# Two graph edge sums: a one-column memset on GpSimd ahead of each gather, and semaphores counted once per four slots

## The chip, the cores and the metric

The kernel runs on one core of a Trainium2 chip. The metric is the device time of one execution in microseconds (us). Before the change three runs took 3500.52, 3505.85 and 3508.72 us; the median is 3505.85 us.

The engines are called by the names of the profile: PE is the matrix engine (PEld its weight loads), DVE the vector engine, ACT the scalar engine, POOL the GpSimd engine, SP the engine that only issues transfers here. POOL also issues the indirect DMAs, the transfers that pick rows by an index.

## The reference

A graph of 6250 nodes with 256 features each and 100000 weighted edges goes through four parts. Cut to what matters here:

```
edge_index = stack([src, dst])
x = x + gnn0(layernorm(x))     # segment_sum(w * (ln(x) @ W)[dst], src), batch norm, relu
x = x + ffn0(layernorm(x))     # top-k tokens through a gelu MLP
x = x + gnn1(layernorm(x))     # segment_sum(w * ln(x)[dst], src) + ln(x), MLP, row norm
x = x + ffn1(layernorm(x))     # mixture of 8 experts, 2 per token
```

The two edge sums are the two `segment_sum`s: for each of 100000 edges a row of 256 floats is fetched by the edge's one end, multiplied with the edge's weight, and added to the row of its other end.

## The kernel before, in words

**Chunks and slots.** The 6250 nodes are 49 tiles (`NT`) of 128 rows. The edges are sorted by the tile that they add to and cut into 784 chunks (`CHUNKS`) of 128 edges. A chunk whose edges belong to two tiles has to be used twice, so there are 832 slots (`SLOTS`): one slot is one chunk's part for one tile. Both edge sums run through `aggregate`, the first with `through_mlp` false (its buffers and semaphores are named `g0_`), the second with it true (`g1_`). Every loop in it is unrolled when the program is built. What the trace calls `g_...` is either.

**What each engine does.** POOL issues one indirect DMA for each chunk (line 1089): 128 rows of 1 KB from the table in HBM into one place of `got`, a ring of 56 places (`RING`). DVE makes for each slot a 128x128 matrix `route` that holds the edge's weight in the column of its target row (line 1098). PE multiplies `route` with the chunk's rows into half of a PSUM bank (line 1182; an f32 product is two MATMUL records in the trace). DVE adds that half bank to the tile's row in `A` (line 1115). 16 slots (`GB`) make a step, in four groups of four (`GSEM`). After each step about one tile is complete, and ACT, PE and DVE take it through what follows: in the first sum a product and column statistics, in the second an MLP, two norms and router scores. There are 52 steps (`STEPS`).

**What sets the order.** Each engine runs its own list of instructions in order, and semaphores tie the lists together. `gathered` tells PE that four chunks have landed. `routed` tells PE that four matrices are made. `pairs_summed` counts each second product on PE: DVE waits for it before it adds, and POOL waits for it before it overwrites a place of the ring. `added` counts each addition: DVE waits for it before its next addition, since two slots can add to the same tile, PE waits for it before it reuses a half bank, and ACT waits for it before it takes a finished tile. PE may run at most 14 slots (12 in the second sum) ahead of the additions.

**The ring's wait.** Chunk c takes the place of chunk c-56. A chunk can still be used up to 48 slots after its own number, so before gathers c and c+1 POOL waits until the products of all slots up to c-7 are done (`last_user`, `done`). The wait is carried by a semaphore instruction of its own (`pool.sem_inc(dma_open, 1)`), once for every two gathers. From chunk 56 on it counts; for chunks 32 and up there is another wait because the eight `gathered` semaphores are reused.

Of the kernel before, what the change touches and what calls it, by code (L numbers as in the profile page):

```python
# [5 lines left out]
ALU = mybir.AluOpType  # L6
# [4 lines left out]
U32 = mybir.dt.uint32  # L11
# [3 lines left out]
P = 128  # L15
# [3 lines left out]
NT = -(-N // P)  # L19
# [64 lines left out]
def wait(engine, sem, value):  # L84

    if not (isinstance(value, int) and value <= 0):
        engine.wait_ge(sem, value)


def build(nc, x, src, dst, edge_weight, g0_w, g0_bias, g0_gamma, g0_beta, f0_wr_in, f0_br, f0_w1, f0_b1_in, f0_w2, f0_b2_in,  # L90
# [14 lines left out]
    with ctx:  # L105
        def sem(name):
            return ctx.enter_context(nc.semaphore(name))
# [5 lines left out]
        dma_open = sem("indirect_dma_open")  # L113
# [897 lines left out]
        def aggregate(rows, name, through_mlp, source, local, weight):  # L1011
# [3 lines left out]
            BANKS = 6 if through_mlp else 7  # L1015
            GROUPS_OF = GB // GSEM
            FINISHES = STEPS - 1
            with ExitStack() as scope, nc.Block() as block:
                here = lambda what, shape, dt=F32: sb(name + what, shape, dt, scope)
                got = here("got", [P, RING, D])  # L1020
                route = here("route", [P, GB + GSEM, P])
                added = sem(name + "added")
                routed, pairs_summed = sem(name + "routed"), sem(name + "pairs_summed")
                tiles_of = GraphTiles(here) if through_mlp else NodeRows(here)
                edges = None if through_mlp else EdgeFields(here)

# [4 lines left out]
                def first_slot_after(q):  # L1031

                    return next(first for first in range(0, SLOTS, GSEM) if landed_by(first) >= q)
# [41 lines left out]
                @block.gpsimd  # L1075
                def _(pool):
                    for q in range(CHUNKS // GSEM):
                        if not through_mlp and q * GSEM in (0, 4 * P):
                            pool.wait_ge(edges.sources_made, 1 + (q > 0))
                        for half in range(2):  # L1080
                            first = q * GSEM + half * (GSEM // 2)
                            last_user = first + GSEM // 2 - 1 - RING + (NT - 1)
                            done = last_user // 2 + 1 if first >= RING else 0
                            if q >= 8:
                                done = max(done, first_slot_after(q - 8) // 2 + 1)
                            wait(pool, pairs_summed, done)
                            pool.sem_inc(dma_open, 1)
                            for c in range(first, first + GSEM // 2):
                                pool.indirect_dma_start(  # L1089
                                    got[:, c % RING, :], None, rows,  # L1090
                                    bass.IndirectOffsetOnAxis(ap=source[:, c:c + 1].bitcast(U32), axis=0)
                                ).then_inc(gathered[q % 8], 16)

                @block.vector
                def _(dve):
# [6 lines left out]
                    def add_sums(n, g):  # L1102
                        first = n * GB + g * GSEM
                        _, tiles = nc.values_load_multi_w_load_instructions(
                            slot_tile[0:1, first:first + GSEM], engines=(mybir.EngineType.DVE,), min_val=0, max_val=NT - 1,
                            skip_runtime_bounds_check_because="the map is clamped to the tiles")
                        if n + 1 < STEPS:
                            make_routes(n + 1, g)
                        for j in range(GSEM):
                            c = first + j  # L1110
                            to = row(A, tiles[j])
                            if j % 2 == 0:
                                dve.wait_ge(pairs_summed, c // 2 + 1)
                            dve.wait_ge(added, c + 1)
                            dve.tensor_tensor(to, to, sums_of(c), ALU.add).then_inc(added, 1)  # L1115

                    if not through_mlp:
                        edges.make(dve)
# [42 lines left out]
                def _(pe):  # L1161
# [5 lines left out]
                    for n in range(STEPS):  # L1167
                        u = n % 2
                        for g in range(GROUPS_OF):
                            pe.wait_ge(routed, n * GROUPS_OF + g + 1)  # L1170
                            first = n * GB + g * GSEM
                            for q in range(asked[0], landed_by(first) + 1):
                                pe.wait_ge(gathered[q % 8], gathered_after(q))
                            asked[0] = landed_by(first) + 1
                            _, at = nc.values_load_multi_w_load_instructions(
                                slot_ring[0:1, first:first + GSEM], engines=(mybir.EngineType.PE,), min_val=0, max_val=RING - 1,
                                skip_runtime_bounds_check_because="the ring's places are below its size")
                            for j in range(g * GSEM, (g + 1) * GSEM):
                                c = n * GB + j
                                if c % 2 == 0 and c >= 2 * BANKS:  # L1180
                                    pe.wait_ge(added, c - 2 * BANKS + 3)
                                ins = pe.matmul(sums_of(c), route[:, c % (GB + GSEM), :], row(got, at[j % GSEM]), start=True, stop=True)  # L1182
                                if c % 2 == 1:
                                    ins.then_inc(pairs_summed, 1)
                            if through_mlp and n >= 2 and g == 0:
                                tiles_of.second_product(pe, n - 2)
                            if through_mlp and n >= 4 and g == 0:
                                tiles_of.score(pe, n - 4)
                            if n >= 1 and g == 1:
                                tiles_of.turn(pe, n - 1)  # L1190
                            if n >= 1 and g == (3 if through_mlp else 2):
                                tiles_of.first_product(pe, n - 1)
                            if through_mlp and n >= 3 and g == 3:
                                tiles_of.turn_normal(pe, n - 3)
# [17 lines left out]
                def _(act):  # L1212
                    if through_mlp:
                        act.wait_ge(tiles_of.loaded, tiles_of.LOADS * 16)
                    for n in range(1, STEPS):
                        act.wait_ge(added, n * GB + 1)
                        t = tile_to_finish(n, mybir.EngineType.Activation)
                        tiles_of.tile.stage(act, n - 1, t)
                        if through_mlp:
# [15 lines left out]
                    if through_mlp:  # L1235
                        tiles_of.keep_result(act, FINISHES - 1)
                        tiles_of.keep_scores(act, FINISHES - 3, tile_to_finish(FINISHES - 2, mybir.EngineType.Activation))
                        left = last_tile(act)
                        act.wait_ge(added, SLOTS + 1)
                        tiles_of.tile.stage(act, FINISHES, left)  # L1240
                        tiles_of.root_of(act, FINISHES - 1)
                        tiles_of.keep_turned(act, FINISHES)
# [10 lines left out]
                        tiles_of.keep_normal_turned(act, FINISHES)  # L1253
                        tiles_of.keep_scores(act, FINISHES, left)
                    else:
                        act.wait_ge(added, SLOTS + 1)
                        left = last_tile(act)
                        tiles_of.tile.stage(act, FINISHES, left)
                        tiles_of.keep_turned(act, FINISHES)
# [968 lines left out]
```

## Time and profile before

| | before |
|---|---|
| median of 3 timed runs | 3505.85 us |
| the profiled execution, first to last instruction | 3891.6 us |
| PE busy | 2650.3 us |
| DVE busy | 2586.9 us |
| POOL busy | 2179.1 us |
| gathers of both edge sums (line 1089) | 1568, busy 1493.5 us, POOL idle before them 845.0 us |
| first and last gather of both sums start at | 369.8 and 3110.5 us |

The profiled execution is 386 us longer than the median of the timed ones, because recording the trace takes time of its own. Nothing else around its span is told, so the span stands for its own time. A row of a group reads: line, engine, operation, what it writes and reads, how many; behind the first bar the busy time in us and the mean of one in ns; behind the second the engine's idle time just before such instructions and what ended most of it. "issue" is idle time that no semaphore explains, "remote" a semaphore whose giver the trace can't name.

### The profile page before, as it was taken

Reading aid. Unit: us, or ns where it says so; the run is one execution under the profiler, and the core shown is the slowest. Engines: PE = TensorE matmul, PEld = TensorE weight load, DVE = VectorE, ACT = ScalarE, POOL = GpSimd, SP = SyncE. Lnnn points to the kernel's source line nnn. Section 1 sums busy time; section 2 is a strip of 40 time slices with the busy share of each in tenths; the row PEclk is TensorE's granted clock in tenths of the full one; section 3 lists DMA queues with packets and bytes.
Section 4 is the critical chain, followed back from the end, with each engine's and each line's share of the span. In section 5 each row is a group of like instructions: output and inputs, shape, how many; then the busy total and the mean of one; then the engine's idle time right before and its main releaser. Section 6 shows DMA issues by size and latency. Waiting matters only on the chain. (4 is left out here: it accounts for less than half of the span.)

```text
span 3891.6 us, 55224 instructions
## 1 busy us (share of the span) xinstructions
PE 2650.3 (68%) x15016; PEld 2238.8 (58%) x15016; DVE 2586.9 (66%) x6599; ACT 1024.1 (26%) x2120; POOL 2179.1 (56%) x2145
## 2 busy tenths in 40 slices
PE   6886555444454545789946666666666657999998
PEld 4666343333343434689935444444444537999998
DVE  8997655444554555976746566666666677888886
ACT  0021000000000000567501111111111127888886
POOL 1434566666666664335456666666666603666665
PEclk8998777777777777899967777777887768999999
DMA  3011333333333332000133333333333334776775
GB/s 90 4 46 58 102 91 92 91 91 88 91 92 88 92 88 63 12 1 23 55 90 96 96 96 96 96 96 94 98 95 94 95 103 165 216 216 212 213 215 146
DMA packets 164219, 387.69 MB, mean 100 GB/s; under 512 B 46324, under 2 KB 95528, under 8 KB 150561
## 3 DMA queue, kind: packets, MB, share of 16 engines
q0 software_dynamic: 99072, 233.49, 22.0%
q1 hardware_dynamic: 64929, 151.65, 11.4%
q8 instruction: 94, 1.54, 0.2%
q14 instruction: 124, 1.02, 0.1%
HBM read 342.69 MB, written 42.97 MB: 99 GB/s over the span
## 5 line engine op out<-in xcount | busy, mean ns | idle before, releaser
L1089 POOL DMA_INDIRECT g_got<-table,e_source x1568 | 1493.5, 952 | 845.0 <-issue 440.0
L1115 DVE TENSOR_TENSOR A<-A,psum 128x256 f32 x1664 | 698.6, 420 | 876.3 <-remote 532.0
L1182 PE MATMUL psum<-g_got,g_route 128*128 x3328 | 1034.7, 473 | 141.0 <-DMA g_got<-table,e_source 74.2
L1182 PEld LDWEIGHTS psum<-g_got,g_route 128*128 128x128 f32 x3328 | 771.9, 241 | 329.0 <-issue 198.4
L786 PE MATMUL psum<-ident,g_rows 128*128 128x128 f32 x208 | 63.0, 401 | 663.3 <-ACT A L834 410.2
L1098 DVE TENSOR_SCALAR g_route<-columns,e_local,e_weight 128x128 f32<-128x128 f32 x1664 | 471.6, 362 | 17.4 <-issue 12.2
L786 PEld LDWEIGHTS psum<-ident,g_rows 128*128 128x128 f32 x208 | 29.7, 190 | 703.8 <-ACT A L834 505.7
L834 ACT COPY A<-psum 128x256 f32 x52 | 19.3, 372 | 999.4 <-issue 637.4
L369 POOL DMA_INDIRECT records<-rec,place x120 | 120.6, 1005 | 233.7 <-ACT rec L585 159.1
L140 PE MATMUL psum<-e_xt_hi,e_w_hi 128*128 128x256 f32 x832 | 238.2, 286 | 5.4 <-issue 5.2
L1612 POOL TENSOR_TENSOR f_ht_lo<-f_ht,f_ht_hi 128x512 fp32r<-128x512 f32 x100 | 134.2, 1347 | 181.1 <-ACT f_ht_hi L1551 174.6
L140 PE MATMUL psum<-e_w_hi,e_ht_hi 128*128 128x256 f32 x832 | 232.8, 280 | 3.1 <-DVE e_w_lo L2011 3.1
L141 PE MATMUL psum<-e_xt_lo,e_w_hi 128*128 128x256 f32 x832 | 233.8, 281 | 0.0
L142 PE MATMUL psum<-e_xt_hi,e_w_lo 128*128 128x256 f32 x832 | 233.7, 281 | 0.0
L141 PE MATMUL psum<-e_w_lo,e_ht_hi 128*128 128x256 f32 x832 | 232.6, 280 | 0.0
L142 PE MATMUL psum<-e_w_hi,e_ht_lo 128*128 128x256 f32 x832 | 232.4, 279 | 0.0
L655 PE MATMUL psum<-to_row,value 125*48 125x128 f32 x1600 | 199.2, 288 | 40.4 <-DVE to_row L553 35.9
L655 PEld LDWEIGHTS psum<-to_row,value 125*48 125x48 f32 x1600 | 187.8, 131 | 64.3 <-issue 49.2
L1890 POOL DMA_INDIRECT out<-e_y,e_homes x104 | 177.0, 1702 | 63.4 <-POOL e_homes L1886 47.6
L2156 ACT ACTIVATE e_ht<-psum,e_b 128x256 f32<-128x256 f32 x416 | 181.7, 472 | 100.2 <-PE psum L142 100.1
L2017 DVE TENSOR_TENSOR e_ht_lo<-e_ht,e_ht_hi 128x512 fp32r<-128x512 f32 x208 | 138.9, 690 | 52.9 <-ACT e_ht_hi L2160 44.8
L140 PEld LDWEIGHTS psum<-e_xt_hi,e_w_hi 128*128 128x128 f32 x832 | 157.7, 190 | 5.8 <-issue 5.8
(413 smaller groups left out, 5403.5 us busy)
## 6 DMA issues: line engine op xcount, KB each, us to landing
e_w<-in_m_w SPq DMA_DIRECT2D x104, 1024.0 KB, 5.1
g_got<-table,e_source POOLq DMA_INDIRECT x1568
expert_table<-g_normal SPq DMA_DIRECT2D x52, 128.0 KB
table<-xn SPq DMA_DIRECT2D x49, 128.0 KB
X<-in_x SPq DMA_DIRECT2D x1, 6144.0 KB
table<-f_ring SPq DMA_DIRECT2D x24, 256.0 KB, 2.1
out<-X SPq DMA_DIRECT2D x1, 6144.0 KB
f_w<-in_f_w SPq DMA_DIRECT2D x2, 1024.0 KB, 6.5
```

The source lines that it names most:

```text
L140: pe.matmul(to, a_hi, b_hi, start=first, stop=False)
L141: pe.matmul(to, a_hi, b_lo, start=False, stop=False)
L142: return pe.matmul(to, a_lo, b_hi, start=False, stop=last)
L655: ins = pe.matmul(sums_of(u), value[0:EP, u, j, :, :].rearrange("p f c -> p (f c)"), to_row[0:EP, u, j, :], start=j == 0, stop=j == GC - 1)
L1089: pool.indirect_dma_start(got[:, c % RING, :], None, rows, bass.IndirectOffsetOnAxis(ap=source[:, c:c + 1].bitcast(U32), axis=0)).then_inc ...
L1098: ins = dve.tensor_scalar(route[:, (n * GB + j) % (GB + GSEM), :], columns[:], local[:, n * GB + j:n * GB + j + 1], weight[:, n * GB + j:n ...
L1115: dve.tensor_tensor(to, to, sums_of(c), ALU.add).then_inc(added, 1)
L1182: ins = pe.matmul(sums_of(c), route[:, c % (GB + GSEM), :], row(got, at[j % GSEM]), start=True, stop=True)
L1612: pool.tensor_tensor(ht_lo[:, m % 2, of], ht[:, of], ht_hi[:, m % 2, of], ALU.subtract).then_inc(h_split, 1)
L1890: pool.indirect_dma_start(out, bass.IndirectOffsetOnAxis(ap=homes[:, u, j:j + 1].bitcast(U32), axis=0), y[:, u, j, :], None, bounds_check= ...
L2017: dve.tensor_tensor(ht_lo[:, u, of], ht[:, of], ht_hi[:, u, of], ALU.subtract).then_inc(h_split, 1)
L2156: act.activation(ht[:, b * MT:(b + 1) * MT], psum[:, 1 + b % 4, 0:MT], ACT.Gelu, bias=b1[:, one, b]).then_inc(hid_out, 1)
```

## The change

In both edge sums:

- POOL: before each gather `memset` writes 0.0 to one column of a scratch tile `pause` (128 rows, one float each). Each gather has its own column. Nothing reads it. That is 784 memsets in each sum, 1568 in all.
- POOL: the ring's wait and the semaphore instruction that carries it stand once for four gathers. The wait before gathers c to c+3 is for the products up to slot c-5, all of them before the first of the four.
- PE: the products are counted once per four (`groups_summed`) and no longer once per two.
- DVE: it waits once per four additions for the products and for its own last group; between the four additions stands a `drain`, and `added` is counted once per four.
- PE's wait for half banks and ACT's wait for a finished tile are restated in the new unit. The first covers one group, rounded up.

```diff
+                pause = here("pause", [P, CHUNKS])
...
-                        for half in range(2):
-                            first = q * GSEM + half * (GSEM // 2)
-                            last_user = first + GSEM // 2 - 1 - RING + (NT - 1)
-                            done = last_user // 2 + 1 if first >= RING else 0
-                            if q >= 8:
-                                done = max(done, first_slot_after(q - 8) // 2 + 1)
-                            wait(pool, pairs_summed, done)
-                            pool.sem_inc(dma_open, 1)
-                            for c in range(first, first + GSEM // 2):
-                                pool.indirect_dma_start(
+                        first = q * GSEM
+                        last_user = first + GSEM - 1 - RING + (NT - 1)
+                        done = last_user // GSEM + 1 if first >= RING else 0
+                        if q >= 8:
+                            done = max(done, first_slot_after(q - 8) // GSEM + 1)
+                        wait(pool, groups_summed, done)
+                        pool.sem_inc(dma_open, 1)
+                        for c in range(first, first + GSEM):
+                            pool.memset(pause[:, c:c + 1], 0.0)
+                            pool.indirect_dma_start(
...
+                        dve.wait_ge(groups_summed, first // GSEM + 1)
+                        dve.wait_ge(added, first // GSEM + 1)
                         for j in range(GSEM):
-                            c = first + j
                             to = row(A, tiles[j])
-                            if j % 2 == 0:
-                                dve.wait_ge(pairs_summed, c // 2 + 1)
-                            dve.wait_ge(added, c + 1)
-                            dve.tensor_tensor(to, to, sums_of(c), ALU.add).then_inc(added, 1)
+                            if j > 0:
+                                dve.drain()
+                            ins = dve.tensor_tensor(to, to, sums_of(first + j), ALU.add)
+                        ins.then_inc(added, 1)
...
-                                    pe.wait_ge(added, c - 2 * BANKS + 3)
+                                    pe.wait_ge(added, (c - 2 * BANKS + 1) // GSEM + 2)
                                 ins = pe.matmul(sums_of(c), route[:, c % (GB + GSEM), :], row(got, at[j % GSEM]), start=True, stop=True)
-                                if c % 2 == 1:
-                                    ins.then_inc(pairs_summed, 1)
+                            ins.then_inc(groups_summed, 1)
```

POOL in the middle of the first edge sum, before. A row is one gather; what it waits for stands in brackets.

```order
L1089 DMA g_got<-table,e_source 128x256 [waits g0_pairs_summed]
L1089 DMA g_got<-table,e_source 128x256
L1089 DMA g_got<-table,e_source 128x256 [waits g0_pairs_summed]
L1089 DMA g_got<-table,e_source 128x256
L1089 DMA g_got<-table,e_source 128x256 [waits g0_pairs_summed]
```

The same place now:

```order
L1089 MEMSET g_pause 128x1 [waits g0_groups_summed]
L1090 DMA g_got<-table,e_source 128x256
L1089 MEMSET g_pause 128x1
L1090 DMA g_got<-table,e_source 128x256
L1089 MEMSET g_pause 128x1
L1090 DMA g_got<-table,e_source 128x256
L1089 MEMSET g_pause 128x1
L1090 DMA g_got<-table,e_source 128x256
L1089 MEMSET g_pause 128x1 [waits g0_groups_summed]
```

Every gather now has a memset in front of it, and the wait stands ahead of every fourth gather and no longer ahead of every second.

DVE at the first group of the first edge sum, before. ISA is the register instruction that sets the address of the tile to add to.

```order
L1104 TENSOR_LOAD slot_tile
L1098 TENSOR_SCALAR g_route<-columns,e_local,e_weight 128x128 x4
L1115 ISA [waits g0_added,g0_pairs_summed]
L1115 TENSOR_TENSOR A<-A,psum 128x256
L1115 ISA [waits g0_added]
L1115 TENSOR_TENSOR A<-A,psum 128x256
L1115 ISA [waits g0_added,g0_pairs_summed]
L1115 TENSOR_TENSOR A<-A,psum 128x256
L1115 ISA [waits g0_added]
L1115 TENSOR_TENSOR A<-A,psum 128x256
```

The same place now (the drains between the additions are not listed in this view):

```order
L1105 TENSOR_LOAD slot_tile
L1099 TENSOR_SCALAR g_route<-columns,e_local,e_weight 128x128 x4
L1116 ISA [waits g0_added,g0_groups_summed]
L1116 TENSOR_TENSOR A<-A,psum 128x256
L1116 ISA
L1116 TENSOR_TENSOR A<-A,psum 128x256
L1116 ISA
L1116 TENSOR_TENSOR A<-A,psum 128x256
L1116 ISA
L1116 TENSOR_TENSOR A<-A,psum 128x256
```

The instructions stand in the same order; of five semaphore conditions behind the first one none is left.

## Rows read from the trace of the kernel before

**Rows 1.** The page, part 1: busy time of each engine

```profile
PE 2650.3 (68%) x15016; PEld 2238.8 (58%) x15016; DVE 2586.9 (66%) x6599; ACT 1024.1 (26%) x2120; POOL 2179.1 (56%) x2145
```

**Rows 2.** The line of the gathers, L1089: durations min/median/max, idle time before, by releaser

```profile
L1089 POOL DMA_INDIRECT g_got<-table,e_source x1568: 940/946/1200, 369.8 to 3110.5; - x196
...
  issue: 440.0, 1415
  remote: 246.6, 74
```

**Rows 3.** Timeline, all engines, 793 to 812 us: start, length, what, [idle before <-releaser]

```profile
793.60 5.35 PE L1182 MATMUL psum<-g_got,g_route 128*128 x24
...
801.40 0.95 POOL L1089 DMA_INDIRECT g_got<-table,e_source  x1 [0.30 <-issue]
802.66 0.95 POOL L1089 DMA_INDIRECT g_got<-table,e_source  x1 [0.30 <-issue]
806.55 0.98 DVE L1115 TENSOR_TENSOR A<-A,psum 128x256 f32 x2 [9.35 <-remote]
807.20 0.95 POOL L1089 DMA_INDIRECT g_got<-table,e_source  x1 [3.59 <-remote]
```

**Rows 4.** Timeline of POOL, 0 to 6 us: memsets of one column in a row

```profile
0.26 0.10 POOL L2220 MEMSET const-float32-1.0<- 128x1 f32 x1
0.29 0.10 POOL L2220 MEMSET const-bfloat16-1.0<- 128x1 bf16 x1
```

**Rows 5.** Timeline of POOL, 3223 to 3256 us, the expert part's start

```profile
3226.62 1.82 POOL L1903 DMA_INDIRECT e_rows<-expert_table,e_nodes  x1 [0.31 <-issue]
3228.45 0.19 POOL L1899 COPY e_nodes<-node_of 128x2 int32<-128x2 int32 x1
3229.46 0.97 POOL L1903 DMA_INDIRECT e_rows<-expert_table,e_nodes  x1 [0.82 <-POOL e_nodes L1899]
...
3233.93 0.18 POOL L1899 COPY e_nodes<-node_of 128x2 int32<-128x2 int32 x1 [2.25 <-DVE e_xt_lo L2037]
```

**Rows 6.** Groups by line and shape, POOL, the expert part: busy us, mean ns

```profile
L1903 POOL DMA_INDIRECT e_rows<-expert_table,e_nodes x104 | 114.1, 1097 | 62.1 <-POOL e_nodes L1899 45.1 <-issue 16.4 <-DMA out<-e_y,e_homes 0.6
L1899 POOL COPY e_nodes<-node_of 128x2 int32 x47 | 55.4, 1178 | 0.0
```

**Rows 7.** Timeline of POOL where the ring first fills, first and second sum

```profile
463.09 1.03 POOL L1089 DMA_INDIRECT g_got<-table,e_source  x1 [16.41 <-PE psum L1182]
...
473.26 0.94 POOL L1089 DMA_INDIRECT g_got<-table,e_source  x1 [0.33 <-issue]
```

```profile
2040.14 0.94 POOL L1089 DMA_INDIRECT g_got<-table,e_source  x1 [9.83 <-PE psum L1182]
```

**Rows 8.** Timeline, all engines, 474 to 486 us

```profile
477.01 0.95 POOL L1089 DMA_INDIRECT g_got<-table,e_source  x1 [0.30 <-issue]
...
480.35 1.99 PE L1182 MATMUL psum<-g_got,g_route 128*128 x8 [0.92 <-DMA g_got<-table,e_source]
480.97 0.95 POOL L1089 DMA_INDIRECT g_got<-table,e_source  x1 [3.01 <-PE psum L1182]
```

**Rows 9.** Timeline of DVE, 455 to 485 us

```profile
457.07 0.98 DVE L1115 TENSOR_TENSOR A<-A,psum 128x256 f32 x2
458.26 0.98 DVE L1115 TENSOR_TENSOR A<-A,psum 128x256 f32 x2 [0.21 <-DVE A L1115]
...
460.27 0.98 DVE L1115 TENSOR_TENSOR A<-A,psum 128x256 f32 x2
```

**Rows 10.** The line of the additions, L1115, durations min/median/max

```profile
L1115 DVE TENSOR_TENSOR A<-A,psum x1664: 405/420/425, 418.6 to 3147.3; 128x256 f32 x185
```

**Rows 11.** Windows: length, PE, PEld, DVE, ACT, POOL busy (instructions), PE clock, DMA share, GB/s

```profile
700.00:1400.00 700.00, 334.69 (x1304) 272.26 (x1303) 354.03 (x1055) 35.63 (x93) 454.90 (x481) 0.73 0.31 90
2100.00:3000.00 900.00, 594.21 (x2120) 440.33 (x2120) 572.38 (x1803) 98.74 (x353) 587.62 (x613) 0.78 0.33 96
```

**Rows 12.** Groups by line, DVE, 2100 to 3000 us

```profile
L1115 DVE TENSOR_TENSOR A<-A,psum 128x256 f32 x629 | 263.7, 419 | 256.3 <-remote 88.2 <-PE psum L1182 86.1 <-DVE A L1115 27.2
```

More of the change, by code:

```diff
@@ L1020, in aggregate @@
                 got = here("got", [P, RING, D])
+                pause = here("pause", [P, CHUNKS])
                 route = here("route", [P, GB + GSEM, P])
                 added = sem(name + "added")
-                routed, pairs_summed = sem(name + "routed"), sem(name + "pairs_summed")
+                routed, groups_summed = sem(name + "routed"), sem(name + "groups_summed")
                 tiles_of = GraphTiles(here) if through_mlp else NodeRows(here)
@@ L1079, in _ @@
                             pool.wait_ge(edges.sources_made, 1 + (q > 0))
-                        for half in range(2):
-                            first = q * GSEM + half * (GSEM // 2)
-                            last_user = first + GSEM // 2 - 1 - RING + (NT - 1)
-                            done = last_user // 2 + 1 if first >= RING else 0
-                            if q >= 8:
-                                done = max(done, first_slot_after(q - 8) // 2 + 1)
-                            wait(pool, pairs_summed, done)
-                            pool.sem_inc(dma_open, 1)
-                            for c in range(first, first + GSEM // 2):
-                                pool.indirect_dma_start(
-                                    got[:, c % RING, :], None, rows,
-                                    bass.IndirectOffsetOnAxis(ap=source[:, c:c + 1].bitcast(U32), axis=0)
-                                ).then_inc(gathered[q % 8], 16)
+                        first = q * GSEM
[8 more added lines that the diff above has]
+                            pool.indirect_dma_start(
+                                got[:, c % RING, :], None, rows,
+                                bass.IndirectOffsetOnAxis(ap=source[:, c:c + 1].bitcast(U32), axis=0)
+                            ).then_inc(gathered[q % 8], 16)
                 @block.vector
@@ L1215, in _ @@
                     for n in range(1, STEPS):
-                        act.wait_ge(added, n * GB + 1)
+                        act.wait_ge(added, n * GROUPS_OF + 1)
                         t = tile_to_finish(n, mybir.EngineType.Activation)
@@ L1238, in _ @@
                         left = last_tile(act)
-                        act.wait_ge(added, SLOTS + 1)
+                        act.wait_ge(added, SLOTS // GSEM + 1)
                         tiles_of.tile.stage(act, FINISHES, left)
@@ L1255, in _ @@
                     else:
-                        act.wait_ge(added, SLOTS + 1)
+                        act.wait_ge(added, SLOTS // GSEM + 1)
                         left = last_tile(act)
```

## The prediction

> **What bounds the kernel now.** I read the page first. Its busy shares point at PE and DVE, with POOL behind them [rows 1], but they average parts with different limits, so I went to the two edge sums by windows: there DVE is busy 51% and 64%, PE 48% and 66%, POOL 65% in both, and the DMA engines a third [rows 11]. No engine is full, so the waits decide. The line of the gathers tells what POOL does: a gather takes 946 ns, and POOL sits idle 845 us before the 1568 of them [rows 2]. The timeline splits that idle time in two. Between gathers that follow at once there is a gap of 0.30 us, so one starts every 1.25 us, as the first two gathers of the timeline show [rows 3]. On 1415 gathers nothing explains the gap; it belongs to the gather. The rest is waits, some 845 - 1568 x 0.305 = 367 us, and most of it has one form: every 12 to 16 gathers, about once a step, POOL stands still for 3.6 us, and DVE for 9.35 us, until PE's counts arrive, although PE's 24 records for those products end at 798.95 and the wait ends at 806.5 [rows 3].
>
> Are those waits there in a timed run? The profiled execution is 3891.6 - 3505.85 = 386 us longer than the median. The gathers' waits are 367 us. The last quarter of the kernel, the expert part, has PE busy nearly throughout and can't give 386 us back. So I take it that late counts from PE are a cost of recording, and that a timed run goes through both edge sums at POOL's own pace: 1568 x 1.25 = 1960 us of the 3506. The sum below is therefore made against the median, 3505.85, and not against the span: in the profiled execution a slower gather would first eat into the 3.6 us waits.
>
> **The memsets.** 1568 more POOL instructions, each in line ahead of a gather, on the engine that sets the pace. No row has a memset between two gathers, so it is bounded. From above: a one-column memset lasts 0.10 us, and the copy of two columns at 3228.45 starts at the moment the gather before it ends, without the 0.30 us gap, and takes 0.19, as much as one that starts on an idle POOL (0.18) [rows 4, 5]. So a small operation neither hides behind a gather nor pays the gap: it adds its length, and the gap stays with the gather. The gather behind such a copy took 0.97 in place of 0.946 [rows 2, 5]. That gives 0.01 + 0.10 + 0.02 = 0.13 us. From below: of memsets in a row each starts 0.03 us after the last [rows 4], so POOL may be free for the gather after 0.03, which gives 0.04 us. The middle, 0.08 us, is what I take. Wider ends: if the memset fits into the 0.30 us gap and the gather then starts at once, the pair gets 0.30 - 0.10 = 0.20 us shorter; if changing between two kinds of work costs what it seems to cost in the expert part's loop (gathers 1097 ns in the mean against 946, copies 1178 against 190 [rows 5, 6]), it gets 0.15 us to about 0.4 us longer.
>
> The Trainium skill bears on this (GPSIMD Engine Reference, "2.1 Instruction dispatch"): each of GpSimd's eight cores starts the next instruction as soon as its own share of the last is done, and a dispatch costs tens of cycles. By it the memset would cost near the lower end, 0.04 us, and the sum below would be some 60 us smaller. The copy that starts at once agrees with the first half; no row here tells the second for a memset.
>
> How many of them count: the first 56 gathers of each sum run into an empty ring and then wait, 16.41 us and 9.83 us [rows 7], and 56 x 0.08 = 4.5 us of memsets only shortens that wait. 1456 are left, and 1456 x 0.08 = 116 us.
>
> **The coarser waits of POOL.** Before, the wait ahead of gathers c, c+1 reached to slot c-7 and the next to c-5; now the first of four waits to c-5, two slots more, 2.5 us earlier in the stream than it had to. It matters only where POOL is close ahead of PE, from chunk 56 to about 71, four groups. The chain is: last gather of a group starts, its product starts 3.3 us later (477.01 to 480.35), four products take 2.0 to 3.8 us, and the next gather starts 0.6 to 0.8 us after the count [rows 8]: 5.9 to 7.9 us, where five gathers give 6.25 us of cover. A stall of 0 to 1.6 us, four times: 0 to 6 us a sum. Before the same chain with two products less just closed, a gap of 0.33 in place of 0.30 [rows 7]. Later each 17 slots give one chunk more of a lead, and nothing waits. With one group more at the ring's first fill (1 to 3 us) I take 5 us a sum, 10 us in all; ends 2 and 20.
>
> **Counts and drains.** PE gives half as many counts and DVE half as many waits. Two additions last 0.98 us for 2 x 0.42 us, so a wait on one's own count costs 0.14 us, and 0.21 us where PE's count is awaited too [rows 9, 10]. If a drain costs nothing, a group of four gets 0.07 to 0.49 us shorter; if it costs as much as the wait, 0.07 us. None of it is on the path while POOL paces the sums. The first sum's DVE needs 3.2 us for a group of four slots, 457.07 to 460.27 [rows 9], where POOL needs 4.7. In the second sum it is close: 572.4 us busy and about 150 us of its own short gaps over some 40 steps (82 of the 150 before the additions [rows 11, 12]) make 18 us a step, POOL's 15.1 gathers 18.9. DVE is the cover here: if it is gone, the second sum can't run faster than today by more than 0.5 to 0.9 us a step. I cost this part at 0; ends -5 and +5.
>
> On the counts the Trainium skill speaks against a gain (VectorE: DVE Perf Modes, "The DRAIN you can't avoid"): eight copies with a semaphore after each took as long as eight with one after the last. By it the edit gives nothing; the row's 0.07 us between the two kinds of wait would be all there is. Both leave the sum as it is.
>
> **Sum.** 116 + 10 + 0 = 126 us. 3505.85 + 126 = 3632 us, 3.6% more.
>
> **Rivals.**
> 1. *The gap closes.* The 0.30 us before each gather is idle time of POOL that no semaphore explains. If part of it belongs to two gathers meeting back to back, a memset between them takes its place. For it: nothing else in the trace explains the gap. Against it: the copy that starts with no gap and is followed by a gather with a gap again, though that one also waits for a semaphore [rows 5]. With 0.10 us gained of the gap: first sum 728 x 0.10 = 73 us, second at DVE's limit about 21 us (52 steps x 0.4), less 10 for the waits: 3505.85 - 84 = 3422 us. With all 0.20 us: 3350 us.
> 2. *The memset is hidden.* It takes 0 to 0.03 us of POOL's time, as the starts in rows 4 allow, or the second sum runs at DVE's pace. 0 to 44 us plus 10: 3516 to 3560 us.
> 3. *Changing work is dear.* Each switch between memset and gather costs 0.15 to 0.4 us, as the expert part's loop suggests. Against it: the copies outside the loop take 0.18 to 0.19 us right beside gathers [rows 5]. 1512 x 0.2 = 302 us at a likely 0.2: about 3820 us; 4120 at the end.
> The point that decides between slower and not is a memset that adds less than 0 us to the 1.25 us period; at -0.007 us it pays for the coarser waits.
>
> **How the numbers follow.** The forecast's mechanism (0.04 to 0.13 us, 3568 to 3715 us) gets 0.55, rival 1 0.22, rival 2 0.13, rival 3 0.10. The likeliest is 3632 us. The range goes from 3420 to 3715 us: it holds the forecast, rival 2, and the nearer part of rival 1, and leaves out rival 3 and the far part of rival 1, some 0.2. The likeliest case's own range is 3568 to 3715. 0.2% is about what a measurement of this kernel can tell, 7 us. Faster by more: rival 1 and a sliver of 2, 0.23. Within: 0.04. Slower: 0.73.
>
> **What would show it.** In the changed profile: memsets of about 0.10 us right at the end of each gather; the start of one gather to the next 1.29 to 1.38 us where nothing waits (1.25 now); gathers still 0.94 to 0.97 us. POOL's wait of 3.6 us once a step shrinks by 16 x 0.08 = 1.3 us, so that the profiled span grows far less than the timed one, to 3890 to 3960 us. Additions on DVE 0.56 us apart or less. The forecast is wrong if the start-to-start time is below 1.26 us (rival 1 or 2) or above 1.4 us (rival 3), or if it is 1.33 us and the time has not moved: then POOL doesn't pace the timed run, and my reading of the 386 us is what failed.

## The result, and the profile after

The changed kernel takes 3512.83 us (median of 20 runs, 3508.55 to 3519.70). The kernel before takes 3509.59 us beside it (20 runs, 3500.52 to 3512.93). The ratio is 1.0013, with a 95% interval of 1.0007 to 1.0019: slower by 0.13%, some 4 us, which is less than the 0.2% taken as no change. (The ratios here are not the quotients of the two medians, which would be 1.0009 for this pair.) The forecast was 3632 us, with 3568 to 3715 for its own mechanism, and the measured time lies outside that. It lies inside the whole range of 3420 to 3715 us, which was wide enough to hold rival 2 and part of rival 1; a time within 0.2% had been given a chance of 0.04. The outcome is near that of rival 2, the hidden memset, with the cost of the coarser waits left over.

The profiled execution spans 3506.7 us and is one of the timed executions, 3508.55 us by its own clock. So recording adds nothing here that can be seen. One chip used below gives the kernel before 3919 us in timed runs, and its trace looks like that of before; the others give it 3504 to 3510 us. The 3891.6 us of the trace before are therefore most likely real time under such a condition, and not stretched by recording, as the text ahead of the prediction has it. Times are compared on one chip only.

The page of after, part 1, answers to [rows 1]. The instructions are the same but for POOL, which has 1568 more.

```profile
PE 2628.2 (75%) x15016; PEld 2217.2 (63%) x15016; DVE 2598.1 (74%) x6599; ACT 1028.1 (29%) x2120; POOL 2374.8 (68%) x3713
```

Part 5 of the same page, four groups of the edge sums: busy us, mean ns, then the engine's idle time before them.

```profile
L1090 POOL DMA_INDIRECT g_got<-table,e_source x1568 | 1495.3, 954 | 288.3 <-issue 274.2
L1184 PE MATMUL psum<-g_got,g_route 128*128 x3328 | 1086.3, 484 | 651.6 <-DMA g_got<-table,e_source 481.3
...
L1116 DVE TENSOR_TENSOR A<-A,psum 128x256 f32 x1664 | 699.2, 420 | 516.3 <-PE psum L1184 298.2
L1099 DVE TENSOR_SCALAR g_route<-columns,e_local,e_weight 128x128 f32<-128x128 f32 x1664 | 470.9, 362 | 18.0 <-issue 12.7
```

The lines of the gathers and of the memsets answer to [rows 2] (durations min/median/max in ns, first and last start; below, idle time by releaser). First the gathers:

```profile
L1090 POOL DMA_INDIRECT g_got<-table,e_source x1568: 942/949/1186, 369.7 to 2755.4; - x196
...
  issue: 274.2, 1438
  PE psum L1184: 1.5, 8
```

Then the memsets:

```profile
L1089 POOL MEMSET g_pause<- x1568: 99/118/372, 369.0 to 2755.1; 128x1 f32 x196
```

Two things are to be seen. The "remote" idle time of 246.6 us is gone, and the last gather starts at 2755.4 in place of 3110.5. That is not the change's work: the kernel before with nothing but the memsets added shows the same (below, last gather at 2749.6), and so does the kernel before with nothing but POOL's wait edited and no memsets (last gather at 2753.7), both near the time of the kernel before. And the idle time that no semaphore explains fell from 440.0 to 274.2 us while 1568 memsets of 0.12 us came in. The memsets lie inside the old gap. The timeline of POOL shows it, where [rows 3] had two gathers 1.26 us apart (start, length, what, idle before):

```profile
461.09 0.95 POOL L1090 DMA_INDIRECT g_got<-table,e_source  x1 [0.19 <-issue]
462.04 0.12 POOL L1089 MEMSET g_pause<- 128x1 f32 x1
462.35 0.94 POOL L1090 DMA_INDIRECT g_got<-table,e_source  x1 [0.19 <-issue]
```

The memset starts at the gather's end, as forecast. The next gather starts 0.31 us after that same end, as without a memset: 461.09 to 462.35.

Where the ring first fills, the coarser waits show ahead of the first of four gathers (here the waiting instruction is the memset), in the place of [rows 7]:

```profile
440.07 0.10 POOL L1089 MEMSET g_pause<- 128x1 f32 x1 [0.37 <-PE psum L1184]
440.73 0.95 POOL L1090 DMA_INDIRECT g_got<-table,e_source  x1 [0.56 <-issue]
...
445.65 0.10 POOL L1089 MEMSET g_pause<- 128x1 f32 x1 [0.21 <-PE psum L1184]
446.31 0.95 POOL L1090 DMA_INDIRECT g_got<-table,e_source  x1 [0.56 <-issue]
...
451.68 0.10 POOL L1089 MEMSET g_pause<- 128x1 f32 x1 [0.66 <-PE psum L1184]
452.33 0.95 POOL L1090 DMA_INDIRECT g_got<-table,e_source  x1 [0.56 <-issue]
```

Behind a memset that waited, the gather starts 0.56 us after the memset's end and not 0.19. The gather before ran from 438.76 to 439.70, so 440.73 is 1.03 us after its end, where 0.31 is usual. So there are three stalls of 0.7, 0.6 and 1.0 us in the first sum; in the second, at 1840.63 and 1852.63, two of 1.3 and 1.9 us. Together 5.5 us. The 16.41 and 9.83 us that POOL waited before chunk 56 in [rows 7] are gone as well: 0.7 us is left in the first sum and nothing in the second. So the first 56 memsets of a sum have no wait to hide in, and all 1568 count.

DVE at the same kind of place as [rows 9], with a drain between two additions:

```profile
779.92 0.42 DVE L1116 TENSOR_TENSOR A<-A,psum 128x256 f32 x1 [3.42 <-PE psum L1184]
780.51 0.42 DVE L1116 TENSOR_TENSOR A<-A,psum 128x256 f32 x1 [0.17 <-issue]
781.10 0.42 DVE L1116 TENSOR_TENSOR A<-A,psum 128x256 f32 x1 [0.17 <-issue]
```

With a drain the next addition starts 0.17 us after the last, between the 0.14 of a wait on one's own count and the 0.21 of a wait on PE's. A group of four has three such gaps, 0.51 us now and 0.14 + 0.21 + 0.14 = 0.49 us before, so the four semaphore conditions fewer (not five, as the text on the change counts them) buy nothing. Additions start 0.59 us apart, where 0.56 or less had been forecast. The longest wait of DVE near the same place is 3.42 us, where [rows 3] has 9.35. There DVE waited on after PE's 24 product records had ended; here PE's 24 records run from 776.15 to 783.23, and the first addition comes at 779.92, while they still go on. The windows inside the two sums answer to [rows 11]; columns are the length, then busy us and instructions of PE, PEld, DVE, ACT and POOL, the granted clock, the DMA share, GB/s:

```profile
700.00:1340.00 640.00, 411.46 (x1410) 310.67 (x1409) 392.05 (x1148) 39.09 (x102) 547.06 (x1020) 0.79 0.37 105
1800.00:2700.00 900.00, 640.22 (x2535) 491.65 (x2535) 685.25 (x2151) 123.32 (x419) 765.79 (x1423) 0.85 0.39 111
```

POOL has 1020 instructions in 640 us, 510 pairs: one pair each 1.255 us. In the second sum it is one each 1.265 us (1423 instructions in 900 us). Apart from the stalls above, POOL goes at nearly its own pace through both sums.

### The profile page after: what moved, and what is told of

The parts are those of the page before. It is cut to its first block and busy times, and to the rows that moved or that the text cites. A ratio compares the mean times of both kernels' runs of the same rounds, so it can differ in the third digit from the quotient of the medians.

```text
span 3506.7 us, 57232 instructions
## 1 busy us (share of the span) xinstructions
PE 2628.2 (75%) x15016; PEld 2217.2 (63%) x15016; DVE 2598.1 (74%) x6599; ACT 1028.1 (29%) x2120; POOL 2374.8 (68%) x3713
## 5 line engine op out<-in xcount | busy, mean ns | idle before, releaser
L1090 POOL DMA_INDIRECT g_got<-table,e_source x1568 | 1495.3, 954 | 288.3 <-issue 274.2
L1184 PE MATMUL psum<-g_got,g_route 128*128 x3328 | 1086.3, 484 | 651.6 <-DMA g_got<-table,e_source 481.3
L1184 PEld LDWEIGHTS psum<-g_got,g_route 128*128 128x128 f32 x3328 | 761.8, 240 | 896.9 <-issue 771.0
L1089 POOL MEMSET g_pause<- 128x1 f32 x1568 | 198.1, 126 | 29.8 <-POOLq L1270 17.3
L2004 DVE TENSOR_TENSOR e_w_lo<-e_w,e_w_hi 128x2048 fp32r<-128x2048 f32 x52 | 119.2, 2293 | 58.3 <-ACT e_w_hi L2166 57.0
```

The source lines that it names most:

```text
L1089: pool.memset(pause[:, c:c + 1], 0.0)
L1090: pool.indirect_dma_start(got[:, c % RING, :], None, rows, bass.IndirectOffsetOnAxis(ap=source[:, c:c + 1].bitcast(U32), axis=0)).then_inc ...
```

## The experiments

**The memset alone** (kernel before plus the memsets).

```diff
                             for c in range(first, first + GSEM // 2):
+                                pool.memset(pause[:, c:c + 1], 0.0)
                                 pool.indirect_dma_start(
```

> The kernel before with the 1568 memsets alone; waits and counts as before. Theory A (the memset fits into the 0.30 us between two gathers): timed within 0.1% of before, 3506 to 3514 us; one gather starts 1.25 us after the last. Theory B (memset costs about 0.08 us and the coarser counts give as much back): 3590 to 3640 us. For the profiled span: if the memsets ended the 3.6 us waits once a step it is near 3510 us, if the halved counts did it stays near 3890 us, which I think likelier.

Measured 3505.18 us (11 runs) beside 3504.43 us of the kernel before (21 runs, measured together with the first four kernels): ratio 1.0001, 0.9991 to 1.0010. Its line of memsets, then that of its gathers:

```profile
L1090 POOL MEMSET g_pause<- x1568: 98/118/279, 368.8 to 2749.3; 128x1 f32 x196
```

```profile
L1091 POOL DMA_INDIRECT g_got<-table,e_source x1568: 942/946/1174, 369.5 to 2749.6; - x196
```

1568 memsets in front of 1568 gathers cost nothing that can be measured: 0.7 us in all, with an interval of -3 to +3.5 us, or 0.000 us each within 0.002. The gathers have no stall where the ring fills. The span is 3503.3 us, not the 3890 thought likelier; the kernel with the counts alone, next, spans 3500.2. So neither half of the change ended the long waits of the trace before: they were never in these runs.

**The counts alone** (changed kernel without the memsets).

```diff
                         for c in range(first, first + GSEM):
-                            pool.memset(pause[:, c:c + 1], 0.0)
                             pool.indirect_dma_start(
```

> The changed kernel without the memsets; counts once per four, drains. Theory A: timed like before, 3506 to 3516 us, and the 3 us by which the changed kernel is slower is split between this and the memsets. Theory B: 3400 to 3430 us. The profiled span is near 3507 us if the halved counts of PE ended the waits in the trace, near 3890 us if the memsets did.

Measured 3509.00 us, ratio 1.0008, 0.9998 to 1.0017. The stalls where the ring fills are there without memsets:

```profile
440.85 0.95 POOL L1089 DMA_INDIRECT g_got<-table,e_source  x1 [0.93 <-PE psum L1183]
...
446.56 0.94 POOL L1089 DMA_INDIRECT g_got<-table,e_source  x1 [0.91 <-PE psum L1183]
...
452.07 0.94 POOL L1089 DMA_INDIRECT g_got<-table,e_source  x1 [0.80 <-PE psum L1183]
```

The two halves of the change add up, 1.0001 and 1.0008 against 1.0013, and the small loss sits in the second half, though its interval just reaches 1. Which line it is, the kernels with one part alone say further below.

**Four memsets ahead of each gather** (changed kernel).

```diff
-                            pool.memset(pause[:, c:c + 1], 0.0)
+                            for m in range(4):
+                                pool.memset(pause[:, 4 * c + m:4 * c + m + 1], 0)   # pause: 4 * CHUNKS bytes a row
```

> The changed kernel with four one-column memsets (one byte wide) ahead of each gather in place of one. Theory A: four in a row end some 0.19 us after the gather (0.10 + 3 x 0.03), inside the 0.30 us gap: no change against the changed kernel, 3513 us, within 0.2%. If each costs its full length one after another, 0.40 to 0.48 us, 0.1 to 0.2 us a gather stick out: 3660 to 3800 us.

Measured 3583.12 us, ratio 1.0219, 1.0197 to 1.0241: 79 us more than before on that chip. Timeline of POOL:

```profile
699.34 0.95 POOL L1091 DMA_INDIRECT g_got<-table,e_source  x1
700.28 0.20 POOL L1090 MEMSET g_pause<- 128x1 uint8 x4
700.63 0.95 POOL L1091 DMA_INDIRECT g_got<-table,e_source  x1
```

Neither expectation was met: theory A said no change, and the other said 3660 us or more. Four memsets take 0.20 us together, and the gather starts 0.35 us after the last gather's end, 0.15 us after the memsets'. From one gather to the next it is 1.296 us where nothing waits, 0.045 more than 1.251, and 0.045 x 1568 = 71 us of the 79; some 4 are the coarser waits. So there is a point beyond which POOL pays, and one memset is far below it. One memset (four bytes wide) is recorded with 0.12 us and four (one byte wide) with 0.20, so each further one adds 0.03 us. This agrees with the Trainium skill (GPSIMD Engine Reference, "2.1 Instruction dispatch"), by which GpSimd's cores start the next instruction when their own share of the last is done. What decided here is that the gather has a delay of its own that runs meanwhile.

**One long memset ahead of each gather** (changed kernel; a scratch ring of four pieces, with a count of its own).

```diff
-                            pool.memset(pause[:, c:c + 1], 0.0)
+                            wait(pool, paused, c - 3)
+                            pool.memset(pause[:, c % 4, :], 0).then_inc(paused, 1)   # pause: 4 x 784 bytes a row
```

> The changed kernel with a memset of 784 bytes a row ahead of each gather in place of one float (0.7 to 0.8 us if a byte costs what a float costs, 0.25 us if four go at once). Theory A with POOL as the pace of a timed run: a pair takes 0.95 + 0.75 us and up to 0.30 us more, so (0.45 to 0.75) x 1512 = 680 to 1130 us longer than 3513 us. Theory C (POOL does not pace the timed run, the length before the next bound is free): clearly less than 0.45 us a gather, below 4100 us. The start-to-start time of gathers in the trace tells the same.

Measured 4474.49 us, ratio 1.2764, 1.2740 to 1.2788: 970 us more. Timeline of POOL:

```profile
699.93 0.77 POOL L1091 MEMSET g_pause<- 128x784 uint8 x1
700.85 0.95 POOL L1092 DMA_INDIRECT g_got<-table,e_source  x1 [0.16 <-issue]
701.81 0.77 POOL L1091 MEMSET g_pause<- 128x784 uint8 x1
```

The pair lasts 1.876 us, 0.625 more, and 0.625 x 1568 is 980 us. Nearly all of it is in the timed runs, so POOL does pace both edge sums in full: had DVE or PE been the limit, the first part of the addition would have been free. The gather again starts 0.15 us after the memset's end. The rule that fits all of them: a gather starts at the later of 0.305 us after the last gather's end and about 0.15 us after the last small operation's end. It holds where POOL waited for nothing. Behind a memset that had waited the delay was 0.56 us (above), behind the copies of [rows 5] 0.82, and no run tells why. Nor is the 0.15 sharp: in the trace of after some single memsets lasted 0.19 to 0.21 us, and the gather still started 0.09 to 0.12 us after their end, with nothing lost.

**The kernel before once more**, on another chip, to see the long waits of [rows 3] again.

> The kernel before, unchanged, profiled once more. If its 3.6 us waits once a step were a cost of recording that comes with this program, the span is near 3890 us again. If they belonged to that one recording, as the spans of the two half changes (3503 and 3500 us) suggest, it is near 3500 us, without such waits, and gathers start every 1.251 us.

Neither case of the expectation came: the span is near 3890 us again, but so are the timed runs. On that chip the kernel before takes 3919.08 us in 23 of them (3911.78 to 3938.55); the profiled one took 3915.62. Its line of the gathers has the waits:

```profile
L1089 POOL DMA_INDIRECT g_got<-table,e_source x1568: 940/946/1193, 371.2 to 3135.3; - x196
...
  issue: 435.7, 1396
  remote: 284.2, 82
  PE psum L1182: 125.7, 88
```

284.2 + 125.7 = 410 us of idle time ended by PE's counts. Each of those 170 gathers has its gap of 0.305 us in any case, 52 us in all, so 358 us are waits, of the 3919 - 3505 = 414 us that this chip takes longer. From the first gather's start to the last's it is 2764 us here and 2380 in the kernel with the memsets alone: 384 of the 414 lie between these two. The waits are real time there; the traces of the kernels that take 3500 to 3540 us have none of them. The timeline has the pattern of [rows 3] once a step:

```profile
797.90 5.58 PE L1182 MATMUL psum<-g_got,g_route 128*128 x24
...
810.63 0.98 DVE L1115 TENSOR_TENSOR A<-A,psum 128x256 f32 x2 [9.51 <-remote]
811.27 0.94 POOL L1089 DMA_INDIRECT g_got<-table,e_source  x1 [3.75 <-remote]
```

The granted clock in the middle of its two sums was lower too, 0.73 and 0.75 where after had 0.79 and 0.85:

```profile
700.00:1400.00 700.00, 330.75 (x1298) 269.65 (x1296) 350.01 (x1043) 34.48 (x90) 450.94 (x476) 0.73 0.31 90
2100.00:3000.00 900.00, 580.80 (x2088) 436.08 (x2088) 563.80 (x1780) 100.30 (x347) 572.34 (x601) 0.75 0.32 94
```

Whether the lower clock makes the counts late or only goes with it was not settled. Two rows speak against the clock alone. Over the 24 records themselves, 797.90 to 803.50, the granted clock was 0.96, the higher level nearly throughout, and DVE's wait for their counts ended only at 810.63. And the kernel with the long memset was granted 0.67 over 700 to 1800 us and has no such wait on POOL, though its longer pairs give PE more time. The ends of PE's records are modelled, so it isn't certain either that the products were done when the records say so.

**Three memsets ahead of each gather**, first on this chip, then on one where the kernel before takes 3505.68 us (29 runs).

```diff
-                            pool.memset(pause[:, c:c + 1], 0.0)
+                            for m in range(3):
+                                pool.memset(pause[:, 3 * c + m:3 * c + m + 1], 0)   # pause: 3 * CHUNKS bytes a row
```

> The changed kernel with three one-byte-wide memsets ahead of each gather. Four of them took 0.20 us, and the gather started 0.15 us after their end, 0.35 us after the gather before it: +0.045 us each. If the rule is the later of two (0.305 us after the last gather, 0.15 us after the last small operation), three end at 0.17 us and cost 0.02 us a gather: 3535 to 3555 us. If memsets are paid for each by each (0.045 / 4 = 0.011 us), three cost 0.034 us: 3560 to 3570 us.

> The changed kernel with three one-byte-wide memsets ahead of each gather in place of one. By the rule that a gather starts at the later of 0.305 us after the last gather's end and about 0.15 us after the last small operation's end: three memsets of some 0.17 us end 0.17 us after the gather, so the gather starts 0.32 us after it, a period of 1.266 us, +0.015 us x 1512 = +23 us over the changed kernel: 3525 to 3540 us where the changed kernel takes 3510. Rival, that each memset beyond the first costs its own 0.03 to 0.05 us: +0.06 to 0.10 us x 1512 = 90 to 150 us, 3600 to 3660 us. Where the kernel before takes about 3919 us: the period grows alike, the waits take it up, within 10 us of the kernel before.

On the chip with the late counts: 3923.11 us, ratio 1.0011, 0.9999 to 1.0023. The 3535 to 3555 us expected for it were meant for the other condition. A gather started 1.268 us after the last in place of 1.251, but no time that can be measured came of it: what POOL loses in a step it no longer waits. This is the whole change and two more memsets; the change itself wasn't run on that chip. On the other chip: 3534.47 us (4 runs), ratio 1.0084, 1.0070 to 1.0099, 28.5 us more than the changed kernel itself, 3505.97 us beside it. Timeline of POOL there:

```profile
701.59 0.95 POOL L1091 DMA_INDIRECT g_got<-table,e_source  x1
702.54 0.17 POOL L1090 MEMSET g_pause<- 128x1 uint8 x3
702.86 0.95 POOL L1091 DMA_INDIRECT g_got<-table,e_source  x1
```

The memsets end 0.17 us after the gather, the next gather starts at 0.32, 0.15 later, and 0.017 x 1568 = 27 us. The rule forecast 23. By the rival, each memset past the first at its own length, 90 to 150 us would have come. The first expectation's rival, three memsets at 0.011 us each, gave 3560 to 3570 us and is out too.

**DVE's part of the change alone**, on both chips; and **POOL's part alone**, on the second.

```diff
+                        dve.wait_ge(pairs_summed, (first + GSEM) // 2)
+                        dve.wait_ge(added, first // GSEM + 1)
                         for j in range(GSEM):
...
-                            dve.tensor_tensor(to, to, sums_of(c), ALU.add).then_inc(added, 1)
+                            if j > 0:
+                                dve.drain()
+                            ins = dve.tensor_tensor(to, to, sums_of(first + j), ALU.add)
+                        ins.then_inc(added, 1)
```

PE's wait for half banks and ACT's waits are restated in groups of four here, as in the change.

> The kernel before with DVE's part alone: one wait and one count for four additions, drains between them; PE counts every second product and POOL waits for every two gathers as before. If POOL's coarser wait makes the 0.5 to 1 us stalls before gathers 56, 60 and 64 of each sum, they are gone here, and the time is that of before within 0.1% (3500 to 3508 us). If DVE's later start on a group makes the difference, the time stays 3 to 5 us above before and the stalls stay.

> The kernel before with DVE's part of the change alone: one wait and one count per four additions, drains between them; PE's counts and POOL's waits as before, no memsets. Where the kernel before takes about 3505 us: by the theory that POOL paces the sums and its wait alone costs, 3505 us, within 2 us of the kernel before, no stall ahead of gathers 56 to 68 beyond 0.4 us. Rival, that PE gets its banks later and counts later: stalls of 0.5 to 2 us there and 3508 to 3511 us. Where the kernel before takes about 3919 us: same within 5 us by both.

```diff
                         for half in range(2):
                             first = q * GSEM + half * (GSEM // 2)
-                            last_user = first + GSEM // 2 - 1 - RING + (NT - 1)
+                            last_user = q * GSEM + GSEM - 1 - RING + (NT - 1)
```

> The kernel before with one edit: POOL's wait ahead of the first two gathers of a group reaches two slots further, as in the change; PE still counts in pairs, DVE waits and counts as before, no memsets. Where the kernel before takes about 3505 us: by the theory that only this coarser wait costs anything, stalls of 0.5 to 2 us ahead of gathers 56, 60, 64 or 68 of each sum, 3 to 6 us in all, 3508 to 3511 us, as the counts alone gave (3509.0). Rival, that the cost comes from DVE's side (one count per four reaching PE later): no stalls there beyond 0.3 us and 3505 us, within 2 us of the kernel before. Where the kernel before takes about 3919 us: both say the same as before within 5 us, since the waits there are PE's late counts.

This second edit is POOL's part.

DVE's part: 3925.31 us on the chip with late counts, ratio 1.0012, 0.9996 to 1.0028, which tells little there; 3502.15 us on the other, ratio 0.9994, 0.9986 to 1.0003. POOL's part, two more slots in the wait of the first two of four gathers and nothing else: 3513.30 us, ratio 1.0021, 1.0013 to 1.0030. That is 7.6 us more, somewhat above the 3508 to 3511 expected. The two intervals don't meet. POOL's timeline of it, ahead of chunks 56 and 64:

```profile
440.25 0.95 POOL L1089 DMA_INDIRECT g_got<-table,e_source  x1 [1.71 <-PE psum L1182]
...
451.95 0.94 POOL L1089 DMA_INDIRECT g_got<-table,e_source  x1 [1.93 <-PE psum L1182]
```

With DVE's part alone the gathers of the same stretch follow at 0.30 us all the way:

```profile
440.21 0.94 POOL L1089 DMA_INDIRECT g_got<-table,e_source  x1 [0.30 <-issue]
...
452.71 0.99 POOL L1089 DMA_INDIRECT g_got<-table,e_source  x1 [0.30 <-issue]
```

Less 0.30 the stalls are 1.4 and 1.6 us, and 0.9 and 1.4 in the second sum, 5.3 us in the trace, inside the 4.6 to 10.5 us of the interval. So the loss is POOL's coarser wait. The rival, that DVE's single count reaches PE late, is out: with that count and the old wait no gather stalls. PE's halved counts were not run by themselves.

**The changed kernel again**, beside these three.

> The changed kernel unaltered, beside the others on one chip. Where the kernel before takes about 3505 us: +4 us, 3508 to 3511 us, ratio 1.0007 to 1.0019. Where the kernel before takes about 3919 us (PE's counts late once a step): the theory that memsets are free and POOL's wait is the only cost says same within 5 us, 3914 to 3926 us; the rival, that with half as many counts from PE the late ones hold POOL longer, says slower by one or two gathers a step, 1.25 to 2.5 us x about 98 steps = 120 to 245 us.

3505.97 us (11 runs) beside 3505.68: ratio 1.0007, 0.9998 to 1.0016. The ratio is at the low end of what was expected and the median below it, and the interval overlaps the first result. On this chip the whole change costs less than POOL's part alone, 7.6 us; the intervals (-0.7 to 5.6 us and 4.6 to 10.5 us) just overlap, and whether the rest of the change gives some of it back is open. The one ratio below 1, DVE's part alone, isn't told from 1.

## Why the prediction was wrong, step by step

- **POOL sets the pace of a timed run, 1.25 us a gather: right.** After has one pair each 1.255 us, and of the long memset's 980 us 970 arrived in the time.
- **The reason given for it, that late counts are a cost of recording: wrong.** They are real on a chip where the kernel takes 3919 us. The trace before and the timed runs before most likely belonged to two such conditions, and the 386 us between them were the warning. That the forecast was made against the median and so wasn't harmed by it is luck in part: the right choice rested on a wrong reason. The forecast of a span of 3890 to 3960 us did fail: it is 3506.7.
- **The memset adds 0.08 us, 1456 times, 116 us: this is the step that failed.** It adds 0.000 +- 0.002 us. The reading of [rows 5] was half right. A small operation does start at the gather's end, without the gap; but from this it was concluded that "it adds its length, and the gap stays with the gather". The gap stays, only it is counted from the last gather's end and runs while the memset does. The row that misled was the copy at 3228.45, whose next gather waited for the copy's semaphore and so showed nothing of the gap. The lower bound, 0.04 us, was too high as well; only rival 2, 0 to 0.03 us, has the value. The rule of the Trainium skill cited beside it (GPSIMD Engine Reference, "2.1 Instruction dispatch") put the cost near the low end, which was the better side. The count of 1456 was off as well: it took the first 56 gathers of each sum to run into waits of 16.41 and 9.83 us [rows 7], and no run at 3500 to 3540 us has these; at no cost a memset it changed nothing.
- **The coarser waits, 5 us a sum, 10 in all: right in place and kind, somewhat large.** 2.3 and 3.2 us in the trace of after; 7.6 us timed for that edit by itself, with an interval of 4.6 to 10.5. It is the one part of the change whose cost can be told from nothing.
- **Counts and drains at 0, within 5 us: right.** Gaps of 0.17 us between additions against 0.14 and 0.21; DVE's part alone -2 us by its ratio, interval -4.9 to +1. The rule of the Trainium skill (VectorE: DVE Perf Modes, "The DRAIN you can't avoid"), by which fewer counts buy nothing, agrees with these numbers.
- **Rival 1, the gap closes: wrong.** The start-to-start time is 1.251 us with a memset and without.
- **Rival 3, changing work is dear: wrong.** Where nothing waits, even four memsets cost 0.045 us. The long copies of the expert part [rows 6] belong to that loop; what makes them long wasn't looked into.
- **Rival 2, hidden, 3516 to 3560 us: the case that came**, a little below its bottom of 10 us over the kernel before, because the coarser waits cost 4 us and not 10. At 0.13 it was underrated. The gap of 0.30 us that "nothing explains" was taken as idle time to be won or kept; that it was a delay in which POOL can do other work was the third reading, and it deserved the largest share.

## What to carry to other kernels

A gap before an instruction that no semaphore explains can be a place to put small work on that engine for nothing: look for an instance where something stands in the gap without a dependence of its own before pricing an insertion. Between back-to-back indirect gathers on POOL there are some 0.15 us of such room in this kernel. When the profiled execution and the timed ones differ by 10%, find out by what rows before building on either; and when a wait is made coarser for fewer instructions, look for its price where the buffer first fills: here it was paid there and not in the steady state.

## What the runs showed of the hardware

- A 128-row gather of 1 KB rows takes 0.95 us on POOL and the next starts 0.305 us after its end. Up to about 0.15 us of memsets in between change nothing; beyond that three (0.17 us) add 0.017 us and four (0.20 us) 0.045.
- One POOL memset of one column takes 0.12 us behind a gather, three take 0.17, four 0.20, and one of 784 bytes a row 0.77.
- The long memset slowed DVE. This is the `route` line in the kernel with it, where the changed kernel has a mean of 362 ns:

```profile
L1101 DVE TENSOR_SCALAR g_route<-columns,e_local,e_weight 128x128 f32<-128x128 f32 x624 | 400.4, 957 | 2.9 <-issue 1.1
L1118 DVE TENSOR_TENSOR A<-A,psum 128x256 f32 x620 | 269.3, 434 | 400.8 <-PE psum L1186 320.8 <-issue 79.9
```

  The additions, which read PSUM, went from 420 to 434. The memset itself kept its 0.77 us. The Trainium skill (SBUF — State Buffer, "Who interferes with whom") has VectorE and GpSimd share one pair of SBUF ports; where a VectorE instruction runs in a mode that uses both pairs, as `tensor_scalar` can, whoever issues first holds the shared pair for its whole instruction. The trace agrees in that the `route` instruction slows and shows VectorE as the one that loses. The size isn't explained: the memsets run 0.77 of every 1.876 us, and shut out for that share alone `route` would take 362 / (1 - 0.41) = 614 ns, an estimate, where 957 were measured. With one-column memsets nothing of it is seen, 362 ns as before. DVE still sat idle 400 us before its additions in that window of 1100, 321 of them until PE's products, so the time of that kernel is POOL's.
- Two chips ran the same kernel in 3505 and 3919 us, each steady within 1%. The longer one has waits of 3.6 us on POOL and 9.5 us on DVE once a step, for counts of products that PE's records show as done, and a lower granted clock. What causes them stays open.
